# Score work of an attention and expert layer regrouped from couples to blocks of three products

## The chip, the cores and the metric

The kernel runs on one core of a Trainium2 chip. The metric is device time in microseconds (us) of one execution. TensorE does matrix products, ScalarE activations and copies, VectorE reductions and elementwise work, GpSimd elementwise work as well, and SyncE issues most of the transfers. In rows of the profile they are PE (PEld for its weight loads), ACT, DVE, POOL and SP.

## The reference, cut to what matters

The input is 8 batches of 512 rows of 128 numbers. Each batch is normalised, goes through attention with 16 heads of width 8, and through a layer of 32 routed experts (6 chosen per row) and one shared expert; both results are added to the input.

```python
xn = layernorm(x)
q, k, v = rope(xn @ Wq.T), rope(xn @ Wk.T), xn @ Wv.T     # 16 heads of 8
scores = einsum('bhqd,bhkd->bhqk', q, k) / sqrt(8)
att = einsum('bhqk,bhkd->bhqd', softmax(scores), v)
h = square(relu(einsum('th,eih->tei', xn, up_w))) * combine[:, :, None]
moe = einsum('tei,ehi->th', h, down_w)
shared = square(relu(xn @ shared_up.T)) @ shared_down.T
out = x + att + moe + shared
```

All is float32. The softmax subtracts the maximum of each row of scores, so the scores of a head are formed twice: once with queries on the partitions, to get the row maxima, and once transposed, with keys on the partitions, where the maximum is taken off and the exponent follows.

## The kernel before

**Units.** The work is a row of 128 units, 16 for each batch. Unit `u` has one group of four heads (`QUAD`) and one tile of 128 keys. For each of its four heads it forms a *transposed score*: a product called max (`weights_max`, `ones` times three bf16 parts of the negated maxima, tile `m_rows`) and on top of it in the same bank the product of keys and queries (`weights_product`). ScalarE takes the exponent of the bank into `probs`. Then `pv` multiplies `probs` with `v_aug`. A unit also has one slice of two experts: `expert_up` (tile `up`), a relu on ScalarE (`relu_out`), gate and square on GpSimd (`gating`, tile `g`), and two units later `expert_down` into the bank `acc`. So `pv`, up and down each stand once in a unit.

**Score tiles.** Row maxima for later units come from *score tiles*: one matmul of 128 queries of one head by 512 keys into one of three banks `sc0` to `sc2`, and one reduction on VectorE (`row_max`, L930). There are 512 of them. When the 16 tiles of a step (four heads, four tiles of queries) are read, GpSimd cuts the maxima into three bf16 parts (`cut_max`), TensorE turns them (`max_transpose`), ScalarE copies them and a transfer lays them into `m_rows`.

**Tiling of the array.** A head's keys and queries take 32 partitions, so four heads use four row groups of TensorE, and matmuls on different row groups run side by side (the profile's form 32\*128, or 3\*128 for max). `pv`, up, down and nearly all side work use four groups of 32 output columns instead (128\*32); some side work uses the whole array (128\*128).

**Order.** The order is written out by hand for every engine. On TensorE a unit is: `couple(u, 0)`, that is max, max, product, product of heads 0 and 1 and then up to two score tiles of other heads; `pv(u-1)`; `couple(u, 1)`; `side_work(u)`; one `expert_down`; `expert_up`. Side work is what the next batches need (transposed input, projections, `v`, shared expert, gates), the turned maxima, and every eighth unit the turned result of the attention.

**Banks.** The transposed scores, up and the side work take turns on a ring of three banks, `st0`, `st1` and `upb` (`ring_order`, `ring_b`). Use number i waits until use i - 3 is read (`bank_free`): a transposed score by its exponent, up by its relu. The waits stand in TensorE's own queue, in front of the first matmul of a use. `probs` and `g` have two buffers, `acc` is one bank, read once per batch by `add_residual` on VectorE, which waits for the last down product of the batch; the first down product of the next batch waits for it (`sum_ready`).

Of the kernel before, what the change touches and what calls it, by code (L numbers as in the profile page):

```python
# [9 lines left out]
ALU = mybir.AluOpType  # L10
# [3 lines left out]
P = 128  # L14
# [39 lines left out]
UP_RING = 3  # L54

TWO_DOWN = (9, 11, 12, 13, 15)
SC_BANKS = 3
# [15 lines left out]
def place_scores():  # L73
    at = TILES + FIRST_AHEAD
    for u in range(UNITS):
# [9 lines left out]
    assert at == TILES * STEPS  # L85


def place_downs():

    done = 0  # L90
    for u in range(FIRST_LAG, UNITS):
        due = u - LAG + 1
# [7 lines left out]
place_scores()  # L100
place_downs()


def build(nc, x, wqT, wkT, wvT, gateT, e_bias, upT, down, shared_upT, shared_down, rope, ident_d,
          expert_rows, head_rows, out):
    ctx = ExitStack()
    with ctx:
# [45 lines left out]
        y = sb("y", [P, 2, T])  # L153
        nmax = sb("nmax", [P, 2, TILES]); n_rest = sb("n_rest", [P, TILES])

# [43 lines left out]
        s_done = sem("s_done"); s_read = sem("s_read")  # L199
        n_step = sem("n_step"); n_cut = sem("n_cut"); m_turned = sem("m_turned"); m_ready = sem("m_ready")  # L200
        t_done = sem("t_done"); probs_ready = sem("probs_ready")
# [62 lines left out]
        def max_column(i):  # L264
            h, qt = head_at(i)
            return h * TT + qt

        def x_of(i):
            return x_first[:, i * TT:(i + 1) * TT, :] if i < FIRST_X else x_next[:]
# [9 lines left out]
        def ring_order():  # L279

            order = []
            for u in range(UNITS):
                b, n, kt, q = u // SLICES, u % SLICES, u % TT, u // TT
                last = u == UNITS - 1
                order += [("st", u * QUAD), ("st", u * QUAD + 1)]
                second = [("st", u * QUAD + 2), ("st", u * QUAD + 3)]
                if last:
                    order += [("up", u)]
                if u >= FIRST_LAG:
                    order += second  # L290
                if kt == ATT_KT and q and q % PAIR == 0:
# [12 lines left out]
                if b + 2 < B:  # L304
# [4 lines left out]
                    if n == K_UNIT:  # L309
                        order += [("qk", 2 * (b + 2) + 1)]  # L310
                if u < FIRST_LAG:
                    order += second
                if not last:
                    order += [("up", u)]
            return order + [("att", STEPS // PAIR - 1)]
# [16 lines left out]
        def cut_max(own, eng, s):  # L332

            own.wait_ge(s_read, (s + 1) * TILES)
            wait(own, m_turned, s)
            src = nmax[:, s % 2, :]
# [282 lines left out]
        def _(act):  # L619
# [150 lines left out]

            for u in range(UNITS):
                b, n, kt, q = u // SLICES, u % SLICES, u % TT, u // TT
                if u:
                    relu_out(u - 1)
# [10 lines left out]
                if u >= FIRST_LAG:  # L785
                    side_out(u)
                if 0 < u <= SLICES:
                    square_relu(u - 1)
            att_evac(STEPS // PAIR - 1)

        @block.vector
        def _(dve):
# [131 lines left out]
            def row_max(tile):  # L924
                s, i = tile // TILES, tile % TILES
                dve.wait_ge(s_done, tile + 1)
                if i == 0:
                    wait(dve, n_cut, s - 1)
                at = max_column(i)
                nc.vector.tensor_reduce(out=nmax[:, s % 2, at:at + 1], in_=sc_b[tile % SC_BANKS][:],  # L930
                                        op=ALU.max, axis=AXX, negate=True).then_inc(s_read, 1)

# [75 lines left out]

            for u in range(UNITS):
                b, n, kt, q = u // SLICES, u % SLICES, u % TT, u // TT  # L1010
                for tile in SC_AT[u, 0]:
                    row_max(tile)
                if b == 0:
                    if n in ROUTE0_MID:
                        route(0, ROUTE0_MID[n])
                    if n in ROUTE1_MID:
                        route(1, ROUTE1_MID[n])
                    if n == STATS_UNIT:
                        stats_of(FIRST_X)
                    if n == AGGR_UNIT:  # L1020
                        moments(FIRST_X).then_inc(var_ready, 1)
                for tile in SC_AT[u, 1]:
                    row_max(tile)
# [4 lines left out]
                if b == 0:  # L1028
                    if n in ROUTE0_END:
                        route(0, ROUTE0_END[n])  # L1030
                    if n in ROUTE1_END:
                        route(1, ROUTE1_END[n])
                if b and b + 1 < B:
                    for piece in ROUTE_AT.get(n, ()):
                        route(b + 1, piece)
                if b and b + FIRST_X < B:
                    if n == STATS_UNIT:
                        stats_of(b + FIRST_X)
                    if n == AGGR_UNIT:
                        moments(b + FIRST_X).then_inc(var_ready, 1)  # L1040
            add_pair(0)
            last_gating()
# [4 lines left out]
        @block.tensor  # L1047
        def _(pe):
            def whole(u):

# [49 lines left out]
            def project(i, w, at=slice(0, T)):  # L1100
                pe.wait_ge(xnT_ready, i + 1)
                if i > 1:
                    bank_free("qk", 2 * i + w)
                m = product(proj_b(i, w), at, (wq, wk)[w], xnT[:, i * T + at.start:i * T + at.stop], COL if i > 2 else P)
                if at.stop == T:
# [99 lines left out]
            def couple(u, k):  # L1205
                for h in (2 * k, 2 * k + 1):
                    weights_max(u, h)
                for h in (2 * k, 2 * k + 1):
                    weights_product(u, h)
                for tile in SC_AT[u, k]:  # L1210
                    score(tile)

            def pv(u):
# [16 lines left out]

            def down_slice(src, weights, first, end, width):
                for t in range(TT):
                    at = slice(t * P, (t + 1) * P)
                    m = product(acc_b, at, src[:, at], weights, width, first and t == 0, end, skip_group_check=True)
                return m

            def expert_down(u, width=P):
# [103 lines left out]

            for u in range(UNITS):
                b, n, kt, q = u // SLICES, u % SLICES, u % TT, u // TT
                couple(u, 0)
# [19 lines left out]
                if u < UNITS - 1:  # L1364
                    expert_up(u, width)
            pv(UNITS - 1)

# [48 lines left out]
```

## Time and profile before

| | |
|---|---|
| time, median of 3 runs | 614.03 us (613.72 to 614.72) |
| the profiled execution | 613.97 us |
| its span in the profile | 612.2 us |
| TensorE busy | 603.6 us (99%) |
| VectorE, ScalarE, GpSimd busy | 427.3, 407.9, 427.7 us |
| TensorE's share of the chain that ended last | 91% |

A row of the timeline gives start, length, engine, line, operation and output<-inputs; matmuls of one kind that follow each other are merged into one row with their number behind the x. A float32 matmul stands there as two records. The lengths of matmuls overlap, since they are pipelined, so what a block costs is read from the start of one block to the start of the next.

### The profile page before, as it was taken

Reading aid. Unit: us, or ns where it says so; the run is one execution under the profiler, and the core shown is the slowest. Engines: PE = TensorE matmul, PEld = TensorE weight load, DVE = VectorE, ACT = ScalarE, POOL = GpSimd, SP = SyncE. Lnnn points to the kernel's source line nnn. Section 1 sums busy time; section 2 is a strip of 40 time slices with the busy share of each in tenths; the row PEclk is TensorE's granted clock in tenths of the full one; section 3 lists DMA queues with packets and bytes.
Section 4 is the critical chain, followed back from the end, with each engine's and each line's share of the span. In section 5 each row is a group of like instructions: output and inputs, shape, how many; then the busy total and the mean of one; then the engine's idle time right before and its main releaser. Section 6 shows DMA issues by size and latency. Waiting matters only on the chain.

```text
span 612.2 us, 19876 instructions
## 1 busy us (share of the span) xinstructions
PE 603.6 (99%) x8123; PEld 271.1 (44%) x8123; DVE 427.3 (70%) x1058; ACT 407.9 (67%) x803; POOL 427.7 (70%) x512
## 2 busy tenths in 40 slices
PE   8999999999999999999999999999999999999997
PEld 7533544444444444444444434444443443444343
DVE  7898965777757776677867777586766877666402
ACT  3578666667666666766667676676667665666664
POOL 5850477677786778867788678876776766667663
PEclk9999999999999999999999999999999999999999
DMA  5175742746436254653437454263545632343430
GB/s 149 37 239 175 163 114 67 233 106 157 110 73 212 67 156 109 198 144 71 122 84 241 106 155 106 49 226 82 139 112 158 188 77 92 86 105 71 106 71 18
DMA packets 52027, 76.17 MB, mean 124 GB/s; under 512 B 5984, under 2 KB 19168, under 8 KB 51936
## 3 DMA queue, kind: packets, MB, share of 16 engines
q1 hardware_dynamic: 51916, 74.90, 46.0%
q8 instruction: 64, 1.05, 0.7%
q14 instruction: 27, 0.22, 0.1%
q10 hardware_dynamic: 20, 0.00, 0.0%
HBM read 56.14 MB, written 18.35 MB: 122 GB/s over the span
## 4 chain that ended last, share of the span: by engine, by line
PE 91%; DVE 4%; DMA 2%; POOL 1%; issue 1%; SPq 1%; ACT 0%; DVEq 0%; POOLq 0%
PE acc L1060 21%; PE pv L1227 20%; PE st L1060 14%; PE upb L1060 10%; PE st L1197 9%; PE sc L1186 5%; PE upb L1197 4%; PE st L1202 3%; DVE nmax L930 3%; PE upb L1202 1%; PE st L1169 1%; DMA k_stack<-qk_parts 1%; DMA stacks<-k_stack 1%; PE upb L1169 1%; PE st L1152 1%
## 5 line engine op out<-in xcount | busy, mean ns | idle before, releaser
L930 DVE TENSOR_REDUCE nmax<-sc 128x1 f32<-128x512 f32 x512 | 328.6, 686 | 143.7 <-PE sc L1186 132.7
L700 ACT ACTIVATE probs<-st 128x512 f32<-128x512 f32 x359 | 202.8, 595 | 29.1 <-PE st L1202 20.3
L558 POOL TENSOR_TENSOR gated<-gate_at,relu 128x512 f32<-128x512 f32 x111 | 142.0, 1279 | 99.7 <-ACT relu L705 90.4
L562 POOL TENSOR_TENSOR g<-gated,relu 128x512 f32<-128x512 f32 x111 | 142.2, 1281 | 16.2 <-POOL gated L558 0.4
L1202 PE MATMUL st<-stacks 32*128 32x512 f32 x359 | 148.7, 578 | 0.0
L1227 PE MATMUL pv<-probs,v_aug 128*32 128x512 f32 x1024 | 136.4, 605 | 0.1
L1060 PE MATMUL acc<-dn,g 128*32 128x128 f32 x3512 | 135.2, 274 | 1.0 <-issue 1.0
L1186 PE MATMUL sc<-stacks 32*128 32x512 f32 x512 | 132.5, 493 | 1.4 <-DVE nmax L930 1.0
L1060 PEld LDWEIGHTS acc<-dn,g 128*32 128x32 f32 x3512 | 112.2, 114 | 23.9 <-issue 23.8
L700 ACT ACTIVATE probs<-upb 128x512 f32<-128x512 f32 x153 | 91.0, 595 | 21.1 <-PE st L1202 13.6
L1197 PE MATMUL st<-m_rows,ones 3*128 3x512 bf16 x359 | 99.4, 385 | 0.2 <-ACT sh L682 0.2
L705 ACT ACTIVATE relu<-st 128x512 f32<-128x512 f32 x71 | 42.4, 597 | 72.8 <-PE st L1060 72.8
L1202 PE MATMUL upb<-stacks 32*128 32x512 f32 x153 | 88.6, 579 | 0.0
L1197 PEld LDWEIGHTS st<-m_rows,ones 3*128 3x128 bf16 x359 | 23.9, 91 | 140.0 <-ACT relu L705 59.5
L1060 PE MATMUL st<-xnT,up 128*32 128x512 f32 (+1 forms) x502 | 73.8, 592 | 0.0
L705 ACT ACTIVATE relu<-upb 128x512 f32<-128x512 f32 x57 | 34.0, 597 | 51.3 <-PE upb L1060 51.3
L1060 PE MATMUL upb<-xnT,up 128*32 128x512 f32 (+1 forms) x354 | 60.1, 595 | 0.3
L1197 PE MATMUL upb<-m_rows,ones 3*128 3x512 bf16 x153 | 58.9, 385 | 0.0
L1186 PEld LDWEIGHTS sc<-stacks 32*128 32x128 f32 x512 | 50.7, 182 | 8.6 <-DVE nmax L930 5.0
L1202 PEld LDWEIGHTS st<-stacks 32*128 32x128 f32 x359 | 50.3, 195 | 0.0
L1197 PEld LDWEIGHTS upb<-m_rows,ones 3*128 3x128 bf16 x153 | 13.9, 91 | 68.4 <-ACT relu L705 40.2
L555 POOL TENSOR_TENSOR g<-gate_at,relu 128x512 f32<-128x512 f32 x16 | 20.4, 1277 | 27.9 <-ACT relu L711 11.3
(188 smaller groups left out, 569.1 us busy)
## 6 DMA issues: line engine op xcount, KB each, us to landing
gate_at<-gate_rows SPq DMA_DIRECT2D x62, 512.0 KB, 6.6
stacks<-q_stack SPq DMA_DIRECT2D x30, 256.0 KB, 6.7
stacks<-k_stack SPq DMA_DIRECT2D x30, 256.0 KB, 6.8
q_stack<-qk_parts SPq DMA_DIRECT2D x28, 256.0 KB, 6.6
k_stack<-qk_parts SPq DMA_DIRECT2D x28, 256.0 KB, 6.0
x_res<-in_x SPq DMA_DIRECT2D x8, 256.0 KB, 7.3
out<-y SPq DMA_DIRECT2D x8, 256.0 KB, 6.9
m_rows<-m_parts SPq DMA_DIRECT2D x95, 4.0 KB
```

Source lines behind the costliest of these rows:

```text
L555: nc.gpsimd.tensor_tensor(g[:, u % 2, :], gate_at[:, group % RING, u % GATES, :], relu[:, u % RELUS, :], ALU.mult).then_inc(g_ready, 1)
L558: nc.gpsimd.tensor_tensor(gated[:, u % 2, :], gate_at[:, group % RING, u % GATES, :], relu[:, u % RELUS, :], ALU.mult).then_inc(gated_read ...
L562: nc.gpsimd.tensor_tensor(g[:, u % 2, :], gated[:, u % 2, :], relu[:, u % RELUS, :], ALU.mult).then_inc(g_ready, 1)
L700: nc.scalar.activation(probs[:, u % 2, h, :], ring_b("st", u * QUAD + h)[:], ACT.Exp).then_inc(probs_ready, 1)
L705: nc.scalar.activation(relu[:, u % RELUS, :], ring_b("up", u)[:], ACT.Relu).then_inc(relu_ready, 1)
L930: nc.vector.tensor_reduce(out=nmax[:, s % 2, at:at + 1], in_=sc_b[tile % SC_BANKS][:], op=ALU.max, axis=AXX, negate=True).then_inc(s_read, 1)
L1060: last = nc.tensor.matmul(to[c:c + n, at], weights[:, c:c + n], moving, start=start, stop=stop, **how)
L1169: m = nc.tensor.transpose(ring_b("att", q)[:, t * P:(t + 1) * P], att_sb[:, t * P:(t + 1) * P], ident[:])
L1186: nc.tensor.matmul(sc_b[tile % SC_BANKS][:], stacks[rows_of(h), s % NQ, 0, qt * P:(qt + 1) * P], stacks[rows_of(h), s % NQ, 1, :], start=T ...
L1197: nc.tensor.matmul(ring_b("st", u * QUAD + h)[:], ones[max_rows_of(h), :], m_rows[max_rows_of(h), u // TT % 2, :], start=True, stop=False)
L1202: nc.tensor.matmul(ring_b("st", u * QUAD + h)[:], stacks[rows_of(h), j, 1, kt * P:(kt + 1) * P], stacks[rows_of(h), j, 0, :], start=False, ...
L1227: m = nc.tensor.matmul(pv_b[h * VW:(h + 1) * VW, :], columns[:, at:at + VW], probs[:, u % 2, h, :], start=kt == 0 and first, stop=kt == TT ...
```

## The change

Units 16 to 123 (from batch 1 on, without the last four) are regrouped. Their 432 transposed scores go in 144 blocks of three, a *triple*, and four triples make a period of three units. In a triple three heads have max and product, and the fourth, the spare head, has one and a half score tiles; the other three heads have half a score tile each, so a triple has three score tiles: one whole in `sc0`, and two made of two halves from two row groups in `sc1` and `sc2`. `triple` writes its matmuls in this order: max a, max b, half, half, product a, product b, the whole tile, max c, product c, half, half. The second halves wait for the first ones (`half_done`), which write the same bank.

Between triples there stand in turn (`unit_at`, `downs_at`): after the first `pv`, side work and up of the period's first unit; after the second two whole down products and nothing else; after the third and after the fourth `pv`, side work and up of one unit and half of a down product each. So `pv` is followed by up or side work, where a couple stood between them.

On the other engines: ScalarE takes three exponents, the side copy and the relu of the same unit after each triple. VectorE reads the three banks of a triple in the order 1, 2, 0 after waiting for all of the triple's tiles, each reduction giving two numbers for two halves, and joins the halves once per step (`n_joined`, from step 5). The other work of VectorE for a unit (`unit_rest`) stands behind its triple's reductions.

```diff
+FIRST_T, LAST_T, PERIOD = SLICES, UNITS - 4, 3
+TRIPLES = (LAST_T - FIRST_T) * QUAD // PERIOD
+    for k in range(TRIPLES):
+        first = FIRST_T * QUAD + k * PERIOD
+        heads = [i % QUAD for i in range(first, first + PERIOD)]
+        spare, = set(range(QUAD)) - set(heads)
+        own = [take(spare) for _ in range(PERIOD)]
...
+        lone = own.pop(0 if own[0][1] % HALVES else -1)
+        triples.append((first, (own[0], [lone, take(heads[0])], [take(heads[2]), take(heads[1])])))
...
+        def unit_at(k):
+
+            return FIRST_T + k // QUAD * PERIOD + (0, None, 1, 2)[k % QUAD] if k % QUAD != 1 else None
+
+        def downs_at(k):
+
+            u = FIRST_T + k // QUAD * PERIOD
+            return ((), ((u - 2, 0), (u - 2, 1), (u - 1, 0), (u - 1, 1)), ((u, 0),), ((u, 1),))[k % QUAD]
...
+            for k, (first, scores) in enumerate(TRIPLE):
+                order += [("st", i) for i in range(first, first + PERIOD)]
+                if unit_at(k):
+                    order += sides(unit_at(k)) + [("up", unit_at(k))]
...
+            def triple_out(k):
+                first = TRIPLE[k][0]
+                for i in range(first, first + PERIOD):
+                    exponent(i // QUAD, i % QUAD)
...
+                side_out(u)
+                relu_out(u)
+                if u % (TT * PAIR) == 0:
+                    att_evac(u // (TT * PAIR) - 1)
...
+            def triple_max(k):
+                dve.wait_ge(s_done, SCORED + (k + 1) * SC_BANKS)
+                dve.wait_ge(n_cut, top_of(k) - 1)
+                places = nmax[:].rearrange("p s e c -> p (s e c)")
+                for bank_at in (1, 2, 0):
+                    low, high = [place_of(half) for half in banks_of(k)[bank_at]]
+                    nc.vector.tensor_reduce(out=places[:, low:high + 1:high - low],
+                                            in_=sc_b[bank_at][:].rearrange("p (e c) -> p e c", e=HALVES),
+                                            op=ALU.max, axis=AXX, negate=True).then_inc(s_read, 1)
...
+            for k in range(TRIPLES):
+                if k < SCORE_TRIPLES:
+                    triple_max(k)
+                if unit_at(k):
+                    unit_rest(unit_at(k))
...
+            def triple(k):
...
+                weights_max(*a)
+                weights_max(*b)
+                if scores:
+                    whole, lone, late = scores
+                    half_score(k, 1, lone[0]).then_inc(half_done, 1)
+                    half_score(k, 2, late[0]).then_inc(half_done, 1)
+                weights_product(*a)
+                weights_product(*b)
+                if scores:
+                    half_score(k, 0, whole, HALVES).then_inc(s_done, 1)
+                weights_max(*c)
+                weights_product(*c)
+                if scores:
+                    pe.wait_ge(half_done, 2 * k + 1)
+                    half_score(k, 1, lone[1]).then_inc(s_done, 1)
+                    pe.wait_ge(half_done, 2 * k + 2)
+                    half_score(k, 2, late[1]).then_inc(s_done, 1)
...
+            for k in range(TRIPLES):
+                triple(k)
+                u = unit_at(k)
+                width = P if u and whole(u) else COL
+                if u:
+                    pv(u - 1)
+                    side_work(u)
+                    expert_up(u, width)
+                for e, part in downs_at(k):
+                    half_down(e, part, width)
```

On TensorE, at the start of batch 1, this stands before: the up product of unit 16 and the two couples of unit 17, with `pv` between them. Rows give line, operation, output<-inputs, shape, and the semaphores that a matmul waits for.

```order
L1060 MATMUL upb<-xnT,up 128x512 [waits probs_ready]
L1197 MATMUL st0<-m_rows,ones 128x512 [waits probs_ready]
L1197 MATMUL st1<-m_rows,ones 128x512 [waits xnT_ready]
L1202 MATMUL st0<-stacks 128x512
L1202 MATMUL st1<-stacks 128x512
L1186 MATMUL sc0<-stacks 128x512 [waits s_read,st_ld2]
L1186 MATMUL sc1<-stacks 128x512 [waits s_read]
L1227 MATMUL pv<-probs,v_aug 32x512 [waits att_ready,probs_ready,v_ready]
L1227 MATMUL pv<-probs,v_aug 32x512 x3
L1197 MATMUL upb<-m_rows,ones 128x512 [waits relu_ready]
L1197 MATMUL st0<-m_rows,ones 128x512 [waits probs_ready]
```

And at the same place now: the up product of unit 16 (it is the first unit of a period) and the whole of the second triple, behind which come the two down products.

```order
L1201 MATMUL st1<-xnT,up 128x512 [waits probs_ready]
L1338 MATMUL upb<-m_rows,ones 128x512 [waits probs_ready]
L1338 MATMUL st0<-m_rows,ones 128x512 [waits xnT_ready]
L1364 MATMUL sc1<-stacks 128x256 [waits s_read]
L1364 MATMUL sc2<-stacks 128x256 [waits s_read]
L1343 MATMUL upb<-stacks 128x512
L1343 MATMUL st0<-stacks 128x512
L1364 MATMUL sc0<-stacks 128x512 [waits s_read]
L1338 MATMUL st1<-m_rows,ones 128x512 [waits relu_ready]
L1343 MATMUL st1<-stacks 128x512
L1364 MATMUL sc1<-stacks 128x256 [waits s_read,half_done]
L1364 MATMUL sc2<-stacks 128x256 [waits s_read,half_done]
```

The matmul that waits for the relu of the up product stood behind a couple and a `pv`; now it is max c of the triple that follows up directly.

On VectorE, at the end of batch 2, this stands before: the last score reductions of unit 49, the read of the attention's result, the sum of the batch, and the next reductions.

```order
L930 TENSOR_REDUCE nmax<-sc0 128x1 [waits s_done]
L930 TENSOR_REDUCE nmax<-sc1 128x1 [waits s_done]
L930 TENSOR_REDUCE nmax<-sc2 128x1 [waits s_done]
L938 RECIPROCAL rec<-st0 128x32 [waits att_turned]
L942 TENSOR_TENSOR att_y<-st0,rec 128x4x32 [waits rec_ready]
L942 TENSOR_TENSOR att_y<-st0,rec 128x4x32
L951 TENSOR_TENSOR y<-acc,x_res 128x512 [waits y_ready,down_done,x_res_ld]
L930 TENSOR_REDUCE nmax<-sc0 128x1 [waits s_done]
```

And now, where unit 49 is the first of its period:

```order
L1047 TENSOR_REDUCE nmax<-sc1 128x2 [waits n_cut,s_done,route_step]
L1047 TENSOR_REDUCE nmax<-sc2 128x2
L1047 TENSOR_REDUCE nmax<-sc0 128x2
L1061 RECIPROCAL rec<-upb 128x32 [waits att_turned]
L1065 TENSOR_TENSOR att_y<-upb,rec 128x4x32 [waits rec_ready]
L1065 TENSOR_TENSOR att_y<-upb,rec 128x4x32
L1074 TENSOR_TENSOR y<-acc,x_res 128x512 [waits y_ready,down_done,x_res_ld]
L1047 TENSOR_REDUCE nmax<-sc1 128x2 [waits n_cut,s_done]
```

The sum (`y<-acc`) stands between the reductions of a period's first and second triple, and the down product that it waits for now stands behind the second triple.

## Rows read from the trace of the kernel before

**Rows 1.** Page, part 1: TensorE's busy time, share of the span, instructions.

```profile
PE 603.6 (99%) x8123; PEld 271.1 (44%) x8123; DVE 427.3 (70%) x1058; ACT 407.9 (67%) x803; POOL 427.7 (70%) x512
```

**Rows 2.** Page, part 4: chain that ended last, shares by engine.

```profile
PE 91%; DVE 4%; DMA 2%; POOL 1%; issue 1%; SPq 1%; ACT 0%; DVEq 0%; POOLq 0%
```

**Rows 3.** Waits of TensorE's matmuls: us in total, times, longest.

```profile
PE sc L1119 <- DVE blank L983: 1.0, 1, 1.0
```

**Rows 4.** Timeline, TensorE, one unit without score tiles or side work.

```profile
587.56 0.39 PE L1197 MATMUL st<-m_rows,ones 3*128 3x512 bf16 x2
...
588.11 1.06 PE L1227 MATMUL pv<-probs,v_aug 128*32 128x512 f32 x8
589.11 0.39 PE L1197 MATMUL upb<-m_rows,ones 3*128 3x512 bf16 x1
...
589.66 1.08 PE L1060 MATMUL acc<-dn,g 128*32 128x128 f32 x32
590.56 1.04 PE L1060 MATMUL st<-xnT,up 128*32 128x512 f32 x8
591.54 0.38 PE L1197 MATMUL upb<-m_rows,ones 3*128 3x512 bf16 x1
```

**Rows 5.** Timeline, TensorE, a couple with two score tiles.

```profile
571.19 0.50 PE L1186 MATMUL sc<-stacks 32*128 32x512 f32 x2
...
571.73 1.07 PE L1227 MATMUL pv<-probs,v_aug 128*32 128x512 f32 x8
```

**Rows 6.** Timeline, TensorE, shared up followed by down, same array form.

```profile
105.24 1.07 PE L1060 MATMUL st<-xnT,sup 128*32 128x512 f32 x8
106.12 1.38 PE L1060 MATMUL acc<-dn,g 128*32 128x128 f32 x44
```

**Rows 7.** Timeline, TensorE, batch 0: pv followed by a 128\*128 transpose.

```profile
33.98 1.06 PE L1227 MATMUL pv<-probs,v_aug 128*32 128x512 f32 x8
34.98 0.66 PE L1097 MATMUL upb<-ident,xn 128*128 128x128 f32 x4
```

**Rows 8.** Timeline, TensorE, batch 0: a late second max, three score tiles.

```profile
46.52 0.52 PE L1197 MATMUL st<-m_rows,ones 3*128 3x512 bf16 x2
46.66 0.61 PE L1202 MATMUL st<-stacks 32*128 32x512 f32 x2
46.98 0.51 PE L1186 MATMUL sc<-stacks 32*128 32x512 f32 x3
47.42 0.64 PE L1227 MATMUL pv<-probs,v_aug 128*32 128x512 f32 x4
```

**Rows 9.** Timeline, all engines, batch 0: a second max held by an exponent.

```profile
56.82 0.62 ACT L700 ACTIVATE probs<-st 128x512 f32<-128x512 f32 x1
...
57.49 0.09 PEld L1197 LDWEIGHTS st<-m_rows,ones 3*128 3x128 bf16 x1 [0.16 <-ACT probs L700]
57.50 0.50 PE L1202 MATMUL st<-stacks 32*128 32x512 f32 x1
...
58.05 0.70 PE L1060 MATMUL upb<-xnT,up 128*128 128x512 f32 x1
```

**Rows 10.** Timeline, all engines: an up product, the next couple, its relu.

```profile
305.27 1.04 PE L1060 MATMUL st<-xnT,up 128*32 128x512 f32 x8
...
306.25 0.38 PE L1197 MATMUL st<-m_rows,ones 3*128 3x512 bf16 x1
...
306.38 0.60 ACT L705 ACTIVATE relu<-st 128x512 f32<-128x512 f32 x1 [0.62 <-PE st L1060]
```

**Rows 11.** Timeline: side work behind a couple, and VectorE's reductions of that couple.

```profile
303.83 0.75 PE L1060 MATMUL upb<-wvg,xnT 128*32 128x160 f32 x16
...
304.00 1.29 DVE L930 TENSOR_REDUCE nmax<-sc 128x1 f32<-128x512 f32 x2 [0.19 <-PE sc L1186]
```

**Rows 12.** Timeline, VectorE, unit 65: attention's result and the batch's sum.

```profile
332.34 0.35 DVE L938 RECIPROCAL rec<-st 128x32 f32<-128x32 f32 x1
...
333.13 0.68 DVE L951 TENSOR_TENSOR y<-acc,x_res 128x512 f32<-128x512 f32 x1
```

More of the change, by code:

```diff
@@ L84, in place_scores, with place_triples, take @@
             left -= n
-    assert at == TILES * STEPS
+    return at
+def place_triples(scored):
+    column = {h: scored // QUAD * HALVES for h in range(QUAD)}
+    triples = []
+    def take(h):
+        n = column[h]
+        if n == TILES * STEPS // QUAD * HALVES:
+            return None
+        column[h] = n + 1
+        return h, n
+    for k in range(TRIPLES):
[3 more added lines that the diff above has]
+        own = [take(spare) for _ in range(PERIOD)]
+        if own[0] is None:
+            triples.append((first, None))
+            continue
+        lone = own.pop(0 if own[0][1] % HALVES else -1)
+        triples.append((first, (own[0], [lone, take(heads[0])], [take(heads[2]), take(heads[1])])))
+    assert all(n == TILES * STEPS // QUAD * HALVES for n in column.values())
+    return triples
 def place_downs():
@@ L91, in place_downs @@
     for u in range(FIRST_LAG, UNITS):
+        if u in range(FIRST_T, LAST_T):
+            done = u - LAG + 1
+            continue
         due = u - LAG + 1
@@ L97, in place_downs @@
             n -= 1
-place_scores()
+SCORED = place_scores()
+TRIPLE = place_triples(SCORED)
+SCORE_TRIPLES = sum(1 for _, scores in TRIPLE if scores)
 place_downs()
@@ L266, in max_column, with quad_of, place_of, banks_of @@
             return h * TT + qt
+        def quad_of(half):
+            return half[1] // (TT * HALVES)
+        def place_of(half):
+            h, n = half
+            return n // (TT * HALVES) % 2 * (HALVES * TILES) + n % HALVES * TILES + h * TT + n // HALVES % TT
+        def banks_of(k):
+            whole, lone, late = TRIPLE[k][1]
+            h, n = whole
+            return ((h, n), (h, n + 1)), sorted(lone, key=place_of), sorted(late, key=place_of)
+        def top_of(k):
+            return max(quad_of(half) for halves in banks_of(k) for half in halves)
+        def reads_of(s):
+            if (s + 1) * TILES <= SCORED:
+                return (s + 1) * TILES
+            last = max(k for k in range(SCORE_TRIPLES) for halves in banks_of(k) for half in halves if quad_of(half) == s)
+            return SCORED + (last + 1) * SC_BANKS
+        def unit_at(k):
[3 more added lines that the diff above has]
+            return ((), ((u - 2, 0), (u - 2, 1), (u - 1, 0), (u - 1, 1)), ((u, 0),), ((u, 1),))[k % QUAD]
         def x_of(i):
@@ L279, in ring_order, with sides @@
         def ring_order():
-            order = []
-            for u in range(UNITS):
+            def sides(u):
                 b, n, kt, q = u // SLICES, u % SLICES, u % TT, u // TT
[L284 to L290, printed above, removed]
+                order = []
                 if kt == ATT_KT and q and q % PAIR == 0:
@@ L1229, in pv, with down_slice @@
                 m.then_inc(pv_done, 1)
-            def down_slice(src, weights, first, end, width):
-                for t in range(TT):
+            def down_slice(src, weights, first, end, width, tiles=range(TT)):
+                for t in tiles:
                     at = slice(t * P, (t + 1) * P)
@@ L1340, in _, with unit @@
             pe.wait_ge(qk32_ready, 2)
-            for u in range(UNITS):
-                b, n, kt, q = u // SLICES, u % SLICES, u % TT, u // TT
+            def unit(u):
                 couple(u, 0)
```

142 lines of the change are left out of this document (107 added, 35 removed).

## The prediction

> **What bounds the kernel now.** I read the engines' busy times first, then the chain that ended last, then TensorE's waits, then the timeline of single units. TensorE is busy 99% of the span, no other engine over 70% [rows 1], and 91% of the chain is TensorE's own work [rows 2]. No wait that stands at a TensorE matmul is longer than 1.0 us [rows 3]. So the time is a sum of TensorE's blocks, and I need what each costs, from start to start. A unit without side work: couple 0.55, `pv` 1.00, couple 0.55, down 0.90, up 0.98, in all 3.98 us (587.56 to 591.54) [rows 4]. A couple with two score tiles takes 0.54 (571.19 to 571.73), so score tiles are free as long as they lie beside the products in other row groups [rows 5]. A column block followed by another of the same form is cheaper: shared up, as large as `pv`, takes 0.88 (105.24 to 106.12) where `pv` before a couple takes 1.00 [rows 4, 6]. Going from column blocks to row blocks thus costs 0.12.
>
> How fast a row block can be: a couple with a late second max shows it. That max began at 46.65 (its row ends at 47.04, one is 0.39 long); behind it came the products and three score tiles, the last in a row group that had done max and product, and `pv` started at 47.42 [rows 8]. Three matmuls after each other in a row group: 0.77; two: 0.55. A round costs 0.22.
>
> **The change, part by part.** All is per period (three units); there are 108 / 3 = 36.
>
> *Column blocks.* Before: 3 x (1.00 + 0.90 + 0.98) = 8.64. Now, after triple 1: `pv` 0.88 and up 0.98, 1.86. After triple 2: two downs, 0.90 each and 0.12 for the way out, 1.92. After triples 3 and 4: `pv` 0.88, up 0.98 - 0.12 = 0.86, half a down with the way out 0.56; 2.30 each. Sum 8.38, a gain of 0.26. Side work goes from behind a couple to behind `pv` at the same price.
>
> *Row blocks, if nothing waits.* Six couples are 3.30. A triple has 2.5 rounds of work in three row groups and 1.5 in the spare one. The order of issue makes it three: max c has to stand behind product a in TensorE's queue, and a late second max did hold back the first row group's product (its row starts at 46.66, with the max, not earlier) [rows 8]. So max c streams in round two, product c in round three: 0.77. Bounds: 0.66, if the row groups ran freely (2.5 rounds), and 0.99, if the first halves take a round of their own. I take 0.80, next to the row that shows three rounds. The halves' waits for `half_done` cost nothing: the first halves were issued two rounds earlier.
>
> *The wait that comes in.* Max c uses the bank of the up product just before it, and waits for its relu. Before, a couple and a `pv` (1.55) stood between up and that wait. From up's start to the relu's start 1.11 us pass (305.27 to 306.38), the relu takes 0.60 [rows 10], and a max held by ScalarE starts 0.05 after it (57.44 to 57.49); from such a max to the next block 0.55 (57.50 to 58.05) [rows 9]. So whatever TensorE does, the block behind the triple starts no earlier than 1.11 + 0.60 + 0.05 + 0.55 = 2.31 after up. Triple 2 follows up directly: 2.31 - 0.98 = 1.33 instead of 0.77. Triples 3 to 4 and 4 to 1 have half a down between: 2.31 - 0.86 - 0.56 = 0.89. Only triple 3, behind two downs, is free of it. Behind the held max stand product c, the last two halves and then all of TensorE's work; VectorE waits as well, since it wants all tiles of a triple. Row blocks: 1.33 + 0.89 + 0.89 + 0.80 = 3.91, a loss of 0.61.
>
> Net +0.35 per period, 36 x 0.35 = +12.6 us.
>
> *Units with whole-array side work.* In 19 of the 108 units (14 turned attention results, 5 transposed inputs) `pv` is followed by a 128\*128 block, and `pv` keeps its 1.00 there [rows 7]: 19 x 0.12 = +2.3.
>
> *The sum of a batch.* `add_residual` waits for the last down of its batch, and the next batch's first down waits for it. In units 49 and 97, firsts of a period, it stands in VectorE's queue before triple 2's reductions, and its down product behind triple 2. From the end of triple 2: down 0.90, reaction 0.17 (303.83 to 304.00) [rows 11], sum 0.68 [rows 12]: 1.75, where the second down was due at 0.90: 0.85 late. Then three reductions (two take 1.29 [rows 11], three about 1.9) end at 3.65, while triple 3 wants the last bank at about 1.75 + 1.02 + 0.25 = 3.0: 0.6 more. 2 x 1.45 = +2.9. In units 17, 65 and 113, seconds of a period, the sum stands behind triple 3's reductions and the attention's result: 0.17 + 1.9 + 0.79 + 0.68 = 3.55 after triple 3 [rows 11, 12], and half a down wants it at 1.00 + about 0.5 + 0.86 = 2.4; less the relu wait that this covers, 1.05 each, +3.1. In the other two batches it is in time.
>
> *At nothing.* VectorE: three reductions end 2.1 us after a triple; the next triple wants the last bank 0.22 into it, 2.1 to 2.5 after, so they just fit; other VectorE work is hidden by the stretch behind the held max, and where it is more it costs as in the batch sums. Should they not fit, see the third rival. ScalarE: twelve exponents and three relus of about 0.6 each [rows 9, 10], 9 us, in periods of 12 us and more. One us goes to side copies that stand before a relu. GpSimd: `gating` of the period's first unit has two downs, triple 3 and `pv` before its product is wanted. Transfers are neither added nor moved against their waits; SyncE's order is unchanged.
>
> Sum: 12.6 + 2.3 + 2.9 + 3.1 + 1 = +21.9. The profiled execution took 613.97 (its span 612.2 and 1.77 around it), 0.06 below the median of the runs: 613.97 + 21.9 = 635.9, say 636 us.
>
> **A rule weighed.** A third matmul in a row group costs 0.22 more than the 0.55 of two, which leaves no room for a weight load of its own [rows 4, 8]. The Trainium skill, "TensorE: Matmul & The Clock Gate", section "Part 3: Packing small matmuls — row/col tiling", says that a weight load overlaps running matmuls only if its row group differs; its section on LDWEIGHTS prices 128 columns at P / 1.2 ns, an estimate of 107 ns. By that rule a triple is about 0.2 longer, 36 x 4 x 0.2 = 29 us more; the trace speaks against it, so it is the fourth rival, and the sum goes by the rows.
>
> **The rivals.**
> 1. *The relu doesn't come last* (faster). All triples take 0.77: 3.08 against 3.30, and 0.26 of column blocks: -0.48 x 36 = -17.3, +2.3 for the 19 units: 599 us. For it: TensorE hardly waits now [rows 3]. Against: the relu would have to be over 0.17 after the triple's start for max c to keep its place at 0.22; rows 10 have it over 0.73 after (306.25 to 306.98). It decides from there: each 0.1 that the relu chain is shorter takes 3 x 36 x 0.1 = 10.8 us off, and no change is reached when it is 0.2 shorter in all three triples. Chance 0.12.
> 2. *In between.* The chain is some 0.2 shorter, or the triples run at 0.66 and the batch sums fit: about 614 us. Chance 0.05.
> 3. *VectorE becomes the bound.* Reductions with two results may take longer; with 0.2 more each they end 0.6 later, which triple 3 pays whole and the next two with 0.2: 1.0 x 36 = 36 more, 672 us. The slack is nil at triple 3, so each 0.1 counts there; against it: the same number of elements is read. Chance 0.07.
> 4. *Weight loads are not hidden in a row group:* 636 + 29 = 665 us. Chance 0.03.
>
> **How the numbers follow.** My forecast has 0.73, its own range 622 to 650: triple 3 between 0.66 and 0.99 is -5 to +7, 0.07 either way in the relu chain is 8, the batch sums may be nothing (-6). To take in the second case and the lower edge of the first the range goes from 612 to 652; rivals 3 and 4 and most of rival 1 stay out, about 0.2. A change of over 0.2% (1.2 us) is about what a measurement of this kernel can tell from none. Faster: 0.13 (rival 1 and a little of 2); same 0.03; slower 0.84.
>
> **What would show it.** In the new profile's waits, TensorE's max (L1338) should be held by ScalarE's relu (L786) some 36 times by about half a us; from an up product to the block behind the triple it should be 2.3 us; `pv` to side work or up 0.88; a triple behind two downs about 0.8; VectorE should be waited for little, but for units 17, 49, 65, 97 and 113. I am wrong if max c starts 0.22 after max a behind an up product, or if periods without side work take under 11.9 us.

## The result, and the profile after

The changed kernel takes 643.49 us (median of 4 runs, 643.21 to 644.8), the kernel before 613.97 in the same comparison: 1.048 times as long, 95% interval 1.0465 to 1.0503. The forecast was 636 us with a range of 612 to 652, slower with a chance of 0.84. The profiled execution took 643.21 us, its span is 641.4, so the span grew by 29.2 where I had summed +21.9.

Busy times, the counterpart of [rows 1]:

```profile
PE 623.2 (97%) x8721; PEld 337.1 (53%) x8721; DVE 436.8 (68%) x1085; ACT 412.5 (64%) x803; POOL 428.3 (67%) x512
```

No engine but TensorE is near the span, and TensorE itself fell from 99% to 97%. That its busy time rose by 20 us says little: a held matmul can lie under others' ends. Waits at TensorE's matmuls, the counterpart of [rows 3] (columns: waiting engine, tile and line, what it waited for, us in total, times, longest):

```profile
PE acc L1201 <- DVE y L1074: 5.3, 5, 1.2
PE upb L1338 <- DVE att_y L1065: 1.5, 2, 0.8
PE st L1338 <- ACT relu L786: 1.5, 9, 0.2
...
PE upb L1338 <- ACT relu L786: 0.6, 4, 0.2
```

The relu stands there with 2.1 us, 13 times. I had said that it would be seen "some 36 times by about half a us", and by this list it hardly is. The timeline shows it all the same. TensorE, ScalarE and VectorE around a second and a third triple (units 40 and 41), to be read from start to start, as in [rows 4, 10]. The products of the row blocks (`stacks`) have one record each here, so x2 is two of them, not one:

```profile
224.28 1.04 PE L1201 MATMUL st<-xnT,up 128*32 128x512 f32 x8
...
225.26 0.38 PE L1338 MATMUL upb<-m_rows,ones 3*128 3x512 bf16 x1
...
225.39 0.60 ACT L786 ACTIVATE relu<-st 128x512 f32<-128x512 f32 x1 [0.17 <-PE st L1201]
225.50 0.39 PE L1364 MATMUL sc<-stacks 32*128 32x512 f32 x1
...
226.04 0.38 PE L1338 MATMUL st<-m_rows,ones 3*128 3x512 bf16 x1
...
226.59 1.95 PE L1201 MATMUL acc<-dn,g 128*32 128x128 f32 x64
226.82 1.89 DVE L1047 TENSOR_REDUCE nmax<-sc 128x2 f32<-128x512 f32 x3 [0.43 <-PE sc L1364]
...
228.48 0.39 PE L1338 MATMUL upb<-m_rows,ones 3*128 3x512 bf16 x1
...
228.77 0.50 PE L1364 MATMUL sc<-stacks 32*128 32x512 f32 x1
228.77 0.39 PE L1338 MATMUL st<-m_rows,ones 3*128 3x512 bf16 x1
...
228.94 0.45 PE L1364 MATMUL sc<-stacks 32*128 32x256 f32 x2
...
229.32 0.64 PE L1404 MATMUL pv<-probs,v_aug 128*32 128x512 f32 x4
```

In the second triple the max of c comes 0.78 after the first max, 0.05 after the relu's end (225.39 + 0.60), and the downs 0.55 behind it: up to downs 2.31 us, which is the predicted chain of 1.11 + 0.60 + 0.05 + 0.55 term by term. Behind two downs (228.48), with no relu to wait for, max c comes after 0.29 and the block takes 0.84. The wait list leaves the held max out for the most part: products a and b (0.57 and 0.58 long, begun at 225.30 and 225.32) still run, so TensorE is not idle while its queue stands. An experiment below, in which nothing runs there, shows the wait.

Medians of all blocks of units 16 to 123, from the starts in the timeline:

| block | predicted | median | mean of 36 (of the fourth: 35) |
|---|---|---|---|
| first triple | 0.89 | 0.90 | 0.96 |
| second triple | 1.33 | 1.34 | 1.38 |
| third triple | 0.80 | 0.84 | 0.93 |
| fourth triple | 0.89 | 0.90 | 0.91 |
| `pv` before a block of its form | 0.88 | 0.88 | |
| two downs before a triple | 1.92 | 1.89 | |

The medians are the forecast. The means are not: single triples, called strays below, are longer by up to 1 us; over all 36 periods the triples lie 6.9 us above their medians. Here is one, the third triple of unit 44's period, all engines:

```profile
239.74 1.28 POOL L639 TENSOR_TENSOR gated<-gate_at,relu 128x512 f32<-128x512 f32 x1
...
239.85 1.32 DVE L1023 TENSOR_TENSOR gates<-tmp,wsum 128x128 f32<-128x128 f32 x1
...
241.10 0.37 DVE L913 BATCH_NORM_AGGREGATE mv<-stats 128x2 f32<-128x6 f32 x4
...
241.39 1.85 DVE L1047 TENSOR_REDUCE nmax<-sc 128x2 f32<-128x512 f32 x3
...
242.00 0.39 PE L1338 MATMUL upb<-m_rows,ones 3*128 3x512 bf16 x1
...
242.69 0.38 PE L1364 MATMUL sc<-stacks 32*128 32x256 f32 x1 [0.15 <-DVE nmax L1047]
...
243.29 0.49 PE L1364 MATMUL sc<-stacks 32*128 32x512 f32 x1
...
243.85 1.07 PE L1404 MATMUL pv<-probs,v_aug 128*32 128x512 f32 x8
```

VectorE has routing and normalisation work of the unit before in its queue (1.32, 0.37) and starts the three reductions at 241.39, 1.28 after the tiles' triple ended (240.11, the start of the downs). Each bank comes free 0.6 after the last, and TensorE takes them at that pace: 1.85 us from 242.00 to `pv` in place of 0.84.

The 1.32 is itself not what that instruction took before, where all eight of its kind had 292 ns in the mean:

```profile
L920 DVE TENSOR_TENSOR gates<-tmp,wsum 128x128 f32<-128x128 f32 x8 | 2.3, 292 | 0.3
```

Here it lies beside an instruction of GpSimd (239.74 to 241.02) and ends 0.15 after it. From unit 16 on, 24 of VectorE's instructions, reductions left out, take over 0.25 us more than the shortest of their kind, and each ends 0.02 to 0.15 after one of GpSimd's that ran beside it. In all they take 21.7 us more than the shortest; in the kernel before it was 6.9 us, in 9 instructions. So VectorE is not only late by its order: instructions of it now fall together with GpSimd's that did not before, and ten of the 24 are the joins, which the change adds. That GpSimd holds them is read from these times; no run moved its work.

The sum of batch 2, the place that the prediction worked out by [rows 11, 12]:

```profile
269.47 1.08 PE L1201 MATMUL acc<-dn,g 128*32 128x128 f32 x32
...
270.68 0.69 DVE L1074 TENSOR_TENSOR y<-acc,x_res 128x512 f32<-128x512 f32 x1 [2.12 <-issue]
...
271.51 1.08 PE L1201 MATMUL acc<-dn,g 128*32 128x128 f32 x32 [0.96 <-DVE y L1074]
...
272.53 0.39 PE L1338 MATMUL st<-m_rows,ones 3*128 3x512 bf16 x1
```

The two downs take 3.06 us instead of 1.89, so +1.17 where I had 0.85, and the next triple, short of banks, 1.24 instead of 0.84, +0.40 where I had 0.6.

### The profile page after: what moved, and what is told of

Read it like the earlier page. It is cut to its first block and busy times, and to the rows that moved or that the text cites. A ratio compares the mean times of both kernels' runs of the same rounds, so it can differ in the third digit from the quotient of the medians.

```text
span 641.4 us, 21466 instructions
## 1 busy us (share of the span) xinstructions
PE 623.2 (97%) x8721; PEld 337.1 (53%) x8721; DVE 436.8 (68%) x1085; ACT 412.5 (64%) x803; POOL 428.3 (67%) x512
## 5 line engine op out<-in xcount | busy, mean ns | idle before, releaser
L1047 DVE TENSOR_REDUCE nmax<-sc 128x2 f32<-128x512 f32 x420 | 264.1, 685 | 141.8 <-PE sc L1364 104.3
L1201 PEld LDWEIGHTS acc<-dn,g 128*32 128x32 f32 (+1 forms) x3824 | 113.3, 111 | 58.2 <-issue 53.5
L1201 PE MATMUL acc<-dn,g 128*32 128x128 f32 (+1 forms) x3824 | 135.1, 274 | 5.3 <-DVE y L1074 5.3
L1364 PE MATMUL sc<-stacks 32*128 32x256 f32 (+1 forms) x700 | 137.7, 380 | 0.6 <-DVE nmax L1047 0.2
L1338 PE MATMUL st<-m_rows,ones 3*128 3x512 bf16 x355 | 107.7, 384 | 3.2 <-ACT relu L786 1.5
L1364 PEld LDWEIGHTS sc<-stacks 32*128 32x128 f32 x700 | 83.9, 182 | 6.5 <-DVE nmax L1047 3.7
L1201 PE MATMUL st<-xnT,up 128*32 128x512 f32 (+1 forms) x536 | 82.5, 595 | 0.1
L786 ACT ACTIVATE relu<-st 128x512 f32<-128x512 f32 x79 | 47.2, 598 | 47.1 <-PE st L1201 46.3
L1034 DVE TENSOR_REDUCE nmax<-sc 128x1 f32<-128x512 f32 x80 | 50.4, 684 | 9.0 <-PE sc L1327 7.5
L1201 PE MATMUL upb<-xnT,up 128*32 128x512 f32 (+1 forms) x320 | 51.9, 596 | 0.2
L786 ACT ACTIVATE relu<-upb 128x512 f32<-128x512 f32 x49 | 29.3, 599 | 26.3 <-PE upb L1201 25.9
```

Of the source, the lines that this page charges most:

```text
L786: nc.scalar.activation(relu[:, u % RELUS, :], ring_b("up", u)[:], ACT.Relu).then_inc(relu_ready, 1)
L1034: nc.vector.tensor_reduce(out=nmax[:, s % 2, 0, at:at + 1], in_=sc_b[tile % SC_BANKS][:], op=ALU.max, axis=AXX, negate=True).then_inc(s_re ...
L1047: nc.vector.tensor_reduce(out=places[:, low:high + 1:high - low], in_=sc_b[bank_at][:].rearrange("p (e c) -> p e c", e=HALVES), op=ALU.max ...
L1201: last = nc.tensor.matmul(to[c:c + n, at], weights[:, c:c + n], moving, start=start, stop=stop, **how)
L1338: nc.tensor.matmul(ring_b("st", u * QUAD + h)[:], ones[max_rows_of(h), :], m_rows[max_rows_of(h), u // TT % 2, :], start=True, stop=False)
L1364: return nc.tensor.matmul(sc_b[bank_at][:, to:to + size], stacks[rows_of(h), s % NQ, 0, qt * P:(qt + 1) * P], stacks[rows_of(h), s % NQ, 1 ...
```

## Experiments

**Theories.** *A:* the median of a triple is set by the relu chain, and the strays by VectorE, which has too little room. *B:* the order of issue or the banks' ring sets them, or the strays come from ScalarE. The kernel before took 613.43 us beside the first four runs and 614.01 beside the last two (7 executions each).

**Half the relu.** Takes the relu of 256 of the 512 columns of `up`; the gating uses them twice.

```diff
+n = T // 2 if FIRST_T <= u < LAST_T else T
-nc.scalar.activation(relu[:, u % RELUS, :], ring_b("up", u)[:], ACT.Relu)
+nc.scalar.activation(relu[:, u % RELUS, 0:n], ring_b("up", u)[:, 0:n], ACT.Relu)
```

> In units 16 to 123 the relu reads only the first 256 of the up product's 512 columns, and GpSimd gates these twice; the relu of the other 256 columns is left out. Theory (the relu's end releases max c): the relu goes from 0.60 to about 0.38 us, so the triple behind an up product alone goes from 1.34 to about 1.12, the triples behind half a down from 0.90 to about 0.82 (max c then waits for the order of issue instead), the triple behind two downs stays at 0.84: 36 x (0.22 + 0.08 + 0.08) = 14 us less, about 630. Rival (the triple is long by itself, by its eleven matmuls and their weight loads): all four lengths stay, 643 us.

Measured 640.69 us, 1.0436 (1.0414 to 1.0458) of before, where about 630 was expected. Timeline, the same second triple as above:

```profile
225.76 0.38 PE L1344 MATMUL upb<-m_rows,ones 3*128 3x512 bf16 x1
...
225.90 0.39 ACT L792 ACTIVATE relu<-st 128x256 f32<-128x256 f32 x1 [0.17 <-PE st L1207]
...
226.34 0.38 PE L1344 MATMUL st<-m_rows,ones 3*128 3x512 bf16 x1
...
226.89 0.32 PE L1207 MATMUL acc<-dn,g 128*32 128x128 f32 x4
```

The relu is 0.21 shorter, max c comes 0.20 earlier after the first max (0.58), and the triple takes 1.13. The medians of the four are 0.84, 1.13, 0.85 and 0.84: together 0.33 less, 12 us over 36 periods. That the relu sets the medians is shown. The time fell by only 3. The means are 0.89, 1.20, 1.01 and 0.85: the strays grew from 6.9 us to 10.5, third triples of 1.7 and 1.9 us among them, so the triples as a whole took 8.5 us less (150.4 to 141.9). The columns took 3 us more and batch 0, where nothing was changed, 1.6; in each of these TensorE's granted clock stood at the lower of its two levels, 1.2 GHz, for 3.4 us: from 29.3 us, with TensorE at work before, and from 500.4, behind a wait of 0.96 us for a batch's sum at 498.0 (0.57 over 500 to 504 us, where `pv` and up took 1.7 each, 1.7 us too much in all). These some 3.3 us are not the relu's; the three other executions, not profiled, had a higher mean clock (0.996 to 0.999 against 0.994) and were slower still, so the 3 us are not explained to the end. What made the strays grow was open after this run; the last two answer it.

**One down behind the first triple, one behind the second.** Two of the four half downs that stood behind the second triple go behind the first one's up product, so that no triple follows an up product directly.

```diff
-return ((), ((u - 2, 0), (u - 2, 1), (u - 1, 0), (u - 1, 1)), ((u, 0),), ((u, 1),))[k % QUAD]
+return (((u - 2, 0), (u - 2, 1)), ((u - 1, 0), (u - 1, 1)), ((u, 0),), ((u, 1),))[k % QUAD]
```

> One of the two whole down products goes from behind the second triple to behind the first one's up product. Theory (relu chain and VectorE's pace together): the second triple, now with a down between up and its max c, falls from 1.34 to about 0.84 (0.50 less), but behind the third gap only one down (1.0) is left, while VectorE's three reductions need 2.1 us after a triple: the third triple's whole tile waits about 0.8 us, so it goes from 0.84 to about 1.65. Net +0.3 x 36 = 11 us, about 655. Rival (the relu alone is what costs): the second triple falls to 0.84, the third stays: 36 x 0.5 = 18 us less, about 625.

Measured 649.96 us, 1.0595 (1.0570 to 1.0620): slower than the changed kernel, by 6.5 us where the theory had 11. The second triple is free of the relu and takes 0.84; the third now takes 1.65, together the +0.31 that was expected. The rest of the 11 came back elsewhere: the strays are 3.8 us instead of 6.9, and the columns took 2.1 us less. The third triple's timeline:

```profile
229.12 1.89 DVE L1047 TENSOR_REDUCE nmax<-sc 128x2 f32<-128x512 f32 x3 [0.75 <-PE sc L1364]
...
229.97 0.39 PE L1338 MATMUL upb<-m_rows,ones 3*128 3x512 bf16 x1
...
229.97 0.87 PE L1364 MATMUL sc<-stacks 32*128 32x256 f32 x2
230.47 0.50 PE L1343 MATMUL upb<-stacks 32*128 32x512 f32 x1
...
231.06 0.49 PE L1364 MATMUL sc<-stacks 32*128 32x512 f32 x1
...
231.62 0.64 PE L1404 MATMUL pv<-probs,v_aug 128*32 128x512 f32 x4
```

A triple 1.02 us behind the end of the last finds VectorE at its first of three reductions: the second half tile goes at about 230.46 (the row of both ends at 230.84, one takes 0.38), products a and b, which need no bank of VectorE's, behind it in the queue, and the whole tile at 231.06, after the third reduction (229.12 + 1.89 = 231.01). In this kernel two triples with score tiles can't follow each other faster than VectorE reads three banks; where the relu's wait is taken away, this wait takes its place.

**Max c issued early**, right behind the first halves, ahead of products a and b.

```diff
                     half_score(k, 2, late[0]).then_inc(half_done, 1)
+                weights_max(*c)
                 weights_product(*a)
...
-                weights_max(*c)
                 weights_product(*c)
```

> In a triple max c is issued before products a and b and the whole score tile instead of behind them. Theory (matmuls are issued in order, max c stands behind the whole tile, which waits for its bank's reduction in the third triple): the third triple falls from 0.84 to about 0.75, the other three are held by the relu and stay at 0.90, 1.34, 0.90: 36 x 0.09 = 3 us less, about 640. Rival 1 (c's own row group, with half a tile ahead of its max, sets the length): no change, 643. Rival 2 (products a and b, now held behind max c, come late for their exponents and for VectorE): the held triples grow by 0.2 each, 36 x 3 x 0.2 = 22 us more.

Measured 646.25 us, 1.0526 (1.0502 to 1.0550). The medians, 0.90, 1.34, 0.84 and 0.90, are those of the changed kernel. So the theory's 3 us did not come, and the time is 2.8 us longer. By blocks the profiled execution, 3.6 us longer than that of the changed kernel, has 3.8 in the columns, 1.0 in batch 0 and 1.2 less in the triples. Of the columns 2.5 are the 27 up products behind turned maxima, which start 0.09 later each. In the held triples products a and b now start with max c, so their exponents come later (one 0.89 after its triple's start at 407.34, where it was 0.66), and the up product behind the turned maxima starts 0.05 after one of them ends (at 409.36): rival 2, at about a tenth of its price. From 502.8 to 506.2 us, behind a batch's sum, the granted clock was at its lower level, 1.2 GHz (0.97 over 500 to 550). Timeline of a third triple:

```profile
230.14 0.38 PE L1364 MATMUL sc<-stacks 32*128 32x256 f32 x2
...
230.18 0.58 PE L1343 MATMUL upb<-stacks 32*128 32x512 f32 x1
...
230.37 0.39 PE L1338 MATMUL st<-m_rows,ones 3*128 3x512 bf16 x1
...
230.43 0.49 PE L1364 MATMUL sc<-stacks 32*128 32x512 f32 x1
...
230.60 0.45 PE L1364 MATMUL sc<-stacks 32*128 32x256 f32 x2
...
230.98 0.64 PE L1404 MATMUL pv<-probs,v_aug 128*32 128x512 f32 x4
```

Max c, issued before product a, starts at 230.37, product a at 230.18: a matmul whose row group is busy (here with its half tile, begun at 230.14) does not hold those of other groups behind it. In the third triples max c starts 0.24 after the first max in the median, where it was 0.29 behind the whole tile, and the block is as long as it was. So its place in the queue held max c by 0.05 at most and didn't set the block, and the step "max c has to stand behind product a" was wrong. The 0.84 stands on the chain that is the same in both: the second halves start 0.46 after the triple's start and last 0.38. Whether that 0.46 is the product ahead of them in their row group or the wait for `half_done` was not tried.

**Sum earlier.** The sum of the batch, for units 17, 65 and 113, ahead of the third triple's reductions.

```diff
-if n == SUM_UNIT and b:
+if n == SUM_UNIT and b and (u - FIRST_T) % PERIOD != 1:
...
+if k % QUAD == 2 and unit_at(k) % SLICES == SUM_UNIT:
+    add_residual(unit_at(k) // SLICES - 1)
```

> In units 17, 65 and 113 VectorE adds the batch's sum before the reductions of the third triple instead of behind them and the attention's result. Theory (the first down of the next batch waits there for the sum): the columns behind the third triple fall by about 1.25 us in these three units and nothing else changes: 3.8 us less, about 640. Rival (VectorE is as late anyway, or the reductions behind the sum hold the next triple): 643, the loss moves to the fourth triple of these periods.

Measured 641.43 us, 1.0452 (1.0429 to 1.0475), 2 us less than the changed kernel, where the theory had 3.8 and the rival nothing: each is true in part. TensorE's waits, from 5.3 to:

```profile
PE acc L1203 <- DVE y L1074: 1.9, 2, 1.0
```

The three stretches between third and fourth triple fell from 4.20, 4.37 and 4.19 to 2.89 each, 4.1 us; the fourth triples behind them rose from 0.84 each to 1.14, 1.56 and 1.18, 1.4 us, since their reductions are now the late ones. The cost is VectorE's queue, and a part of it is moved, not taken away.

**Half the reductions.** The triples' reductions read 2x128 columns of a bank, so the maxima leave out half the columns.

```diff
-in_=sc_b[bank_at][:].rearrange("p (e c) -> p e c", e=HALVES),
+in_=sc_b[bank_at][:].rearrange("p (e c) -> p e c", e=HALVES)[:, :, 0:T // 4],
```

> Leaves out the maxima of every second 128 columns: the triples' reductions read 2x128 columns of a bank in place of 2x256, all else as in the changed kernel. Theory: VectorE is what stretches single triples (their means lie above their medians by 6.9 us over the region) and what holds the columns behind the triples at the batch sums (6.1 us, of which the three reductions that stand ahead of the sum are less than half). So the medians of triples 1, 2 and 4 stay at 0.90, 1.34 and 0.90 (the relu), the strays go, and the time is 643.5 - 6.9 - 2.5 = 634 us. Rival: the strays come from ScalarE (its side copies and exponents ahead of a relu) and VectorE only waits beside them; then 641 to 644 us. Beside it, for triple 3 (behind two downs): if VectorE's third reduction sets its 0.84, it falls to about 0.77; if the halves' chain through half_done sets it, it stays.

Measured 636.44 us, 1.0364 (1.0341 to 1.0388): 7 us less than the changed kernel, where the theory had 9 or 10 and the rival 0 to 2. Reductions by line, count, busy us and mean ns, then the same triple that took 1.85:

```profile
L1047 DVE TENSOR_REDUCE nmax<-sc 128x2 f32<-128x256 f32 x420 | 152.3, 419 | 229.8 <-PE sc L1364 165.3 <-issue 59.5 <-DVE gmark L996 2.3
```

```profile
239.78 1.09 DVE L1047 TENSOR_REDUCE nmax<-sc 128x2 f32<-128x256 f32 x3
...
241.50 0.39 PE L1338 MATMUL upb<-m_rows,ones 3*128 3x512 bf16 x1
...
242.34 0.64 PE L1404 MATMUL pv<-probs,v_aug 128*32 128x512 f32 x4
```

The reduction took 419 ns instead of 685, and this triple 0.84. The means are now 0.93, 1.34, 0.83 and 0.90: of 6.9 us of strays some 0.4 is left, which is the very first triple, 1.34 long, since it follows unit 15's up product directly. The medians stay, the relu's at 1.34 and 0.90 too, and the third triple's 0.84, so VectorE doesn't set that one. The columns gave 1 us and not 2.5: the down products behind the batch sums still wait 4.3 us.

**Both halves: relu and reductions.** The two edits above together.

> Leaves out the relu of half the columns of units 16 to 123 (as in the run with half the relu) and the maxima of every second 128 columns. Theory: the half relu alone brought 3 us and not 14 because VectorE took the place of the relu in single triples and at the batch sums. With both relieved all four triples stand at their medians of that run (0.84, 1.125, 0.85, 0.84, or 36 x 3.655 = 131.6 us in place of 141.3), and the batch sums are some 2.5 us cheaper: 640.7 - 9.7 - 2.5 = 628.5 us. Even so not below the 613.4 of the kernel before, since the period is 8.38 + 3.66 = 12.04 us against 11.94. Rival: what ate the gain was something else (the bank ring, ScalarE's exponents); then 638 to 641 us.

Measured 625.12 us, 1.017 (1.014 to 1.020), 18 us less than the changed kernel. The theory had 628.5. Alone the relu brought 3 and the reductions 7. The relu by line (two of the 79 are full ones; the half ones took 384 ns in the mean), and its second triple:

```profile
L792 ACT ACTIVATE relu<-st 128x256 f32<-128x256 f32 (+1 forms) x79 | 30.8, 390 | 45.9 <-PE st L1207 45.1
```

```profile
223.73 0.39 PE L1344 MATMUL upb<-m_rows,ones 3*128 3x512 bf16 x1
...
223.87 0.38 ACT L792 ACTIVATE relu<-st 128x256 f32<-128x256 f32 x1 [0.17 <-PE st L1207]
...
224.30 0.38 PE L1344 MATMUL st<-m_rows,ones 3*128 3x512 bf16 x1
...
224.85 1.96 PE L1207 MATMUL acc<-dn,g 128*32 128x128 f32 x64
```

The means, 0.85, 1.12, 0.83 and 0.86, sum to 3.67 us in a period, near the 3.66 expected. So VectorE did take the relu's place in single triples of the first run, and with both eased nothing else stepped in. In the triples alone the relu brought 8.5 us, the reductions 6.4, both 18.5. And even so the kernel is 11 us slower than before: 3.67 is still more than the 3.30 of six couples, and the columns, with their waits for the batch sums (still 4.3 us), give nothing back; they take 359.9 us where those of the kernel before took 358.4. No version that these runs point to beats the kernel before.

## Why the prediction was right, and what it missed

1. *Column blocks, -0.26 a period:* right in its prices. `pv` took 0.88 before another column block in all its cases, two downs 1.89 for 1.92. The Trainium skill, "TensorEngine Tiling (Array Packing)", section "Key Properties", says that a change of the tiling mode drains the array; the trace agrees and gives the price here, 0.12 (1.00 - 0.88).
2. *The relu chain, 2.31 from up to the block behind the triple:* right in every term (1.11, 0.60, 0.05, 0.55), and the half relu moved the medians by what it took off. Rivals 1 and 2 fell with that.
3. *A free triple, 0.80:* 0.84, inside its bounds of 0.66 to 0.99, 1.6 us over 36 periods. The reason given for it was wrong, so that it came so near is luck: the order of issue doesn't set the block, as max c's early issue showed; the second halves end it. The late max of [rows 8] began 0.05 after an exponent's end (46.01 + 0.59), so it was held by a wait, and a wait does hold what is queued behind it (last section). The Trainium skill, "TensorE: Matmul & The Clock Gate", section "The mechanism", has matmuls start and end in strict program order; here a later one in another row group started 0.19 earlier (230.18 against 230.37), so the measurement decides.
4. *Whole-array side work, 19 units:* right, and 6 units short. Gates' transposes behind `pv` also cost it 1.00, though their rows read 128\*32, 0.7 us in all.
5. *Batch sums, +6.0:* of these 4.8 in the column blocks, where they cost 6.4: 1.17 each behind units 49 and 97 (0.85 expected) and 1.31, 1.48 and 1.30 behind 17, 65 and 113 (1.05 each), which the sum's earlier place took out of these columns. The triples that follow 49 and 97 are counted in the next step.
6. *"VectorE ... just fits", and its other work at nothing:* this is the step that was mis-sized. It fits in the median and not in the periods in which routing, normalisation or the attention's result stands ahead of the reductions, or in which the attention's result frees a bank for max b late (0.8 us, twice). That is nearly all of the 6.9 us; with reductions of 419 ns the first triple's 0.4 remained. The part in it of instructions that lie beside GpSimd's is not measured by a run.

The sum, from the traces, from block to block: the triples take 150.4 us where the couples of the same units took 120.3, so +30.1: medians (3.99 - 3.30) x 36 = +24.7 (22.0 expected), strays +6.9 (1.2 expected behind the batch sums, and 1 for side copies), less 1.5 by which the couples lay above 0.55. The columns, with all their waits, take 359.6 us where it was 358.4, +1.2; the prediction sums -9.4 + 2.3 + 4.8 = -2.3. Of these 3.5 us 1.6 are at the batch sums, 0.8 at the turned maxima (1.3 us instead of 0.5) and 0.7 at the gates. What stands before unit 16 took 106.9 us instead of 108.8, -2.0, though the change leaves it as it was; half of that is a pause of 1.02 us of TensorE in the profiled execution of the kernel before, up to 96.66 us, for which its profile shows no cause. So units 16 to 123 grew by 31.2 us, 9.3 more than the forecast's 21.9 and not 7.5: 5.9 in the triples and 3.5 in the columns, and the 2.0 that made the miss look smaller are luck.

The third rival, VectorE as the bound, was thus partly true: not by slower reductions (one with two results took 685 ns in the mean, one with one result 686 in the kernel before), but by what stands before them. With the relu halved it bounds more single triples, while the medians still fall.

## What to carry to other kernels

When a change puts a consumer right behind its producer, add the whole chain from producer to the block behind the consumer; here it gave the medians of the three triples that it sets to 0.01 us. A wait list can miss such a wait, since matmuls still running cover a held one: measure from block start to block start. And where two engines are each near the pace, ease both before judging a gain, and judge it by the blocks that it touches: in the triples halving the relu brought 8.5 us, the reductions 6.4, both 18.5; in the time of the kernel it was 3, 7 and 18. A new order of one engine also changes which instructions of VectorE and GpSimd lie beside each other: compare the lengths of unchanged instructions, too.

## What the runs showed of the hardware that was not expected

- Matmuls of different row groups start out of the order of issue when the earlier one's row group is busy (230.18 before 230.37). A wait for a semaphore does hold what is queued behind it: with max c issued early, products a and b of a second triple started together with max c, when its relu was done, at 227.70, and not 0.04 after the triple's start. Here nothing covers the wait, and the row of max c carries it (0.38):

```profile
226.91 0.39 PE L1338 MATMUL upb<-m_rows,ones 3*128 3x512 bf16 x1
...
227.70 0.39 PE L1338 MATMUL st<-m_rows,ones 3*128 3x512 bf16 x1 [0.38 <-ACT relu L786]
227.70 0.49 PE L1343 MATMUL upb<-stacks 32*128 32x512 f32 x1
...
228.25 0.54 PE L1201 MATMUL acc<-dn,g 128*32 128x128 f32 x12
```

- The block still ended 1.34 after its start (228.25 - 226.91): the two products lay beside product c at no cost, in other row groups.
- Half the columns don't halve the time: the relu went from 598 to 384 ns, the reduction from 685 to 419.
- An instruction of VectorE's that lies beside one of GpSimd's can take as long as that one is still running: the gates' instruction took 0.29 us, and 1.32 where it ended 0.15 after GpSimd's `gated` (4 of 6 from unit 16 on).
